# Two-layer graph network, one core: the opening's convolution by three half-rate products, weight sums on VectorE, new opening order

## The reference

```python
h = relu(layernorm(x))
c = bn1(conv1d(h^T, conv1_w)); c = relu(c)             # kernel size 1
c = bn2(conv1d(c, conv2_w, pad 8))                     # kernel size 17 along the nodes
x_conv = relu(c + h^T)^T
s = h @ w_se^T + b_se                                  # 3 coordinates a node
A = exp(-squared distances of s within a graph) * adj
x_nmp = A @ relu(h @ w_msg^T + b_msg)
x = x + GRU cell(input [x_conv, x_nmp], state h)       # w_ih, w_hh, gates r, z, n
x = x + adj @ (relu(layernorm(x)) @ L1_weight) + L1_bias
```

## Time and profile before

| | us |
|---|---|
| three runs: median (lowest, highest) | 351.57 (350.06, 353.5) |
| the profiled execution, own time | 351.87 |
| its span | 350.1 |
| busy: PE / DVE / ACT / POOL | 333.0 / 264.1 / 220.9 / 151.7 |

### The profile page before, as it was taken

One profiled execution on the slowest core, in us unless ns is written; L12 is line 12 of the kernel. 1 busy time (PEld: TensorE's weight loads), 2 busy tenths in 40 slices (PEclk: granted clock), 3 DMA queues, 4 the chain that ended last, 5 costly groups with the idle time before them and its releaser, 6 DMA issues.

```text
span 350.1 us, 6296 instructions
## 1 busy us (share of the span) xinstructions
PE 333.0 (95%) x2196; PEld 299.2 (85%) x2196; DVE 264.1 (75%) x733; ACT 220.9 (63%) x431; POOL 151.7 (43%) x130
## 2 busy tenths in 40 slices
PE   7699979999999999999999999999999999999954
PEld 5489868799989998899988998889889998999854
DVE  5597985898688977898679968899577868744672
ACT  2958635876776785677676686587667736352342
POOL 7052470025932297026912495218900593181041
PEclk9999989999999999999999999999999999999988
DMA  6900200001310031001300121002100010000001
GB/s 224 339 3 0 81 11 0 2 1 39 112 33 1 6 116 62 0 2 61 99 24 0 33 92 60 0 2 77 46 0 2 11 51 0 3 30 32 1 1 60
DMA packets 7951, 15.02 MB, mean 43 GB/s; under 512 B 1008, under 2 KB 1648, under 8 KB 7792
## 3 DMA queue, kind: packets, MB, share of 16 engines
q1 hardware_dynamic: 7776, 14.62, 12.2%
q10 hardware_dynamic: 144, 0.01, 0.0%
HBM read 10.43 MB, written 4.19 MB: 42 GB/s over the span
## 4 chain that ended last, share of the span: by engine, by line
issue 40%; POOL 27%; PE 16%; DVE 9%; ACT 6%; DMA 1%; POOLq 0%; ACTq 0%; DVEq 0%
POOL x_ring L1309 4%; POOL base L1321 3%; POOL ac L926 3%; POOL px L930 2%; POOL px L920 2%; POOL px L923 2%; POOL rs L1262 2%; POOL base L1324 2%; POOL rs L1267 2%; POOL base L1315 2%; DVE st L943 1%; DMA x_ring<-x_in 1%; PE pZ L469 1%; PE pQ L329 1%; PE pNR L305 1%
## 5 line engine op out<-in xcount | busy, mean ns | idle before, releaser
L1267 POOL TENSOR_TENSOR rs<-ve,neg_half 128x4 f32<-128x4 f32 x16 | 16.6, 1034 | 100.2 <-DVE ve L1072 100.2
L1262 POOL TENSOR_TENSOR rs<-ve,neg_half 128x8 f32<-128x8 f32 (+1 forms) x9 | 15.5, 1721 | 74.5 <-DVE ve L950 74.5
L303 PE MATMUL pP<-cx_hi,conv_hi 128*128 128x256 f32 x154 | 45.0, 292 | 0.0
L305 PE MATMUL pP<-cx_hi,conv_lo 128*128 128x256 f32 x154 | 43.4, 282 | 0.0
L304 PE MATMUL pP<-cx_lo,conv_hi 128*128 128x256 f32 x154 | 43.3, 281 | 0.0
L303 PE MATMUL pQ<-cx_hi,conv_hi 128*128 128x256 f32 x126 | 37.2, 295 | 0.0
L305 PE MATMUL pQ<-cx_hi,conv_lo 128*128 128x256 f32 x126 | 35.4, 281 | 0.0
L304 PE MATMUL pQ<-cx_lo,conv_hi 128*128 128x256 f32 x126 | 35.4, 281 | 0.0
L720 ACT ACTIVATE work<-work,nb,rs 128x128 f32<-128x128 f32 x60 | 24.8, 483 | 16.1 <-DVE nb L1076 16.1
L303 PEld LDWEIGHTS pP<-cx_hi,conv_hi 128*128 128x128 f32 x154 | 29.1, 189 | 0.3
L304 PEld LDWEIGHTS pP<-cx_lo,conv_hi 128*128 128x128 f32 x154 | 29.1, 189 | 0.3
(11 more groups left out here) (270 smaller groups left out, 1076.0 us busy)
## 6 DMA issues: line engine op xcount, KB each, us to landing
x_ring<-x_in SPq DMA_DIRECT2D x16, 256.0 KB, 2.9
adj_ring<-adj_in SPq DMA_DIRECT2D x16, 256.0 KB, 3.1
out<-x_ring SPq DMA_DIRECT2D x15, 256.0 KB, 2.0
work<-conv_in SPq DMA_DIRECT2D x1, 1088.0 KB, 7.6
x_ring<-gate_in SPq DMA_DIRECT2D x1, 576.0 KB, 7.7
out<-x_ring SPq DMA_DIRECT2D x2, 128.0 KB, 1.7
early<-early_in SPq DMA_DIRECT2D x1, 129.5 KB, 3.2
late<-late_in SPq DMA_DIRECT2D x1, 128.0 KB, 7.9
```

The source lines that it names most:

```text
L303: pe.matmul(acc, w_hi, m_hi, start=start, stop=False)
L305: return pe.matmul(acc, w_lo, m_hi, start=False, stop=stop)
L1262: pool.tensor_tensor(rs1[:, lane], ve1[:, lane], neg_half[:, lane], ALU.pow).then_inc(rs1_set, 1)
L1267: pool.tensor_tensor(rs2[g % 2][:], ve2[g % 2][:], neg_half[:, 0:GG], ALU.pow).then_inc(rs2_set, 1)
```

## The change

**Convolution of groups 0 and 1.** `direct` goes. Three products at half rate take its place, each of eight taps: `even_tap` (even weights on even minus odd phases, into `pQ`), `sum_tap` (sums of even and odd weights on the odd phases, into `pP`), `odd_tap` (odd weights on the next even minus the odd phases, into `pP` again, once `with_sum` has taken the second product's result out of `pP` into `base[0]` and `base[1]`), and tap 16 once for each bank. The differences are made on DVE (`less_odd`, `next_less_odd`), the four pairs of phases split by `split_hi_first(k)` and `split_lo_first(k)`.

**Weights.** `sum_phases` leaves POOL; `sum_odd` (`M21`, 1024 columns) and `sum_halves` (`M12` 1024, `M22` 512) are on DVE. Weights are split in seven parts, not six, in the same total. `W_SUMS` says which sums a part waits for.

**Order.** `opening()` of PE, ACT and DVE is written anew: the fronts of groups 2 and 3 move ahead of much of the convolution; the third product comes last. POOL's `scale1([2, 3])` no longer waits for `cxlo_set` 2, and the sums are gone from between it and `pre`. `split_hi(1, k)` stands in another place and order, `FIRST_ORDER`, and waits for the product that read the place before (`FIRST_FILLS`).

```diff
-        W_PARTS = (taps(8, A0), taps(8, A2), taps(1, T16), taps(4, M22), taps(8, M12), taps(8, M21))
-        W_SUMS = (0, 0, 0, 2, 2, 3)
+        W_PARTS = (taps(4, A0), taps(4, A2), taps(1, T16), taps(8, M21), None, taps(4, M22), taps(8, M12))
+        W_SUMS = (0, 0, 0, 1, 0, 3, 2)
...
-        FIRST_ORDER = (0, 3, 4, 1, 2)
+        FIRST_ORDER = (0, 3, 1, 4, 2)
+        FIRST_FILLS = (None, 3, 4, 0, 4)
...
+            def half_rate(bank, part, w, j, start=False, stop=False):
                 w_hi, w_lo = conv_hi[:, w * D:(w + 1) * D], conv_lo[:, w * D:(w + 1) * D]
+                x = FIRST_AT[part]
+                if j % 2 == 0:
+                    parts = [(bank[:], slice(x, x + 2), j // 2)]
+                else:
+                    parts = [(bank[:, 0:CG * QN], slice(x + 1, x + 2), j // 2),
+                             (bank[:, CG * QN:], slice(x, x + 1), j // 2 + 1)]
...
+            def even_tap(j):
+                return half_rate(pQ, 0, (A0, A2)[j % 2] + j // 2, j, start=j == 0)
+
+            def sum_tap(j):
+                return half_rate(pP, 1, (M21, M23)[j % 2] + j // 2, j, start=j == 0, stop=j == 6)
+
+            def odd_tap(j):
+                return half_rate(pP, 3, (A1, A3)[j % 2] + j // 2, j, start=j == 0)
```

More of the change, by code:

```diff
@@ L494, in opening @@
                 pe.wait_ge(w_split, 1)
-                pe.wait_ge(cxlo_set, 2)
[L496 to L502, removed]
+                pe.wait_ge(cxlo_set, 1)
+                even_tap(0)
+                even_tap(2)
+                even_tap(4)
+                even_tap(6)
+                messages(1)
+                pe.wait_ge(w_split, 2)
@@ L518, in opening @@
+                half_rate(pQ, 2, T16, 8, stop=True).then_inc(f_done[3], 1)
                 conv1(3)
                 neighbour_sums(1)
-                direct(14)
                 messages(3)
                 rows_turn(2)
-                direct(3)
+                pe.wait_ge(w_split, 5)
+                pe.wait_ge(cxlo_set, 4)
+                pe.wait_ge(t0_set, 2)
+                odd_tap(0)
+                odd_tap(2)
+                rows_turn(3)
+                odd_tap(4)
                 distances(2)
-                direct(7)
@@ L526, in opening @@
-                rows_turn(3)
-                direct(11)
+                odd_tap(6)
                 distances(3)
+                odd_tap(1)
+                odd_tap(3)
                 neighbour_sums(2)
[L530 to L536, removed]
+                odd_tap(5)
@@ L537, in opening @@
+                odd_tap(7)
+                half_rate(pP, 1, T16, 8, stop=True).then_inc(f_done[4], 1)
                 gates_h(0)
@@ L838, in opening @@
                 conv_round(0, 0)
+                round_w(5)
+                round_w(6)
+                sums_hi(3)
+                conv_round(0, 1)
                 hidden_gate(0)
-                conv_round(0, 1)
                 first(4)
-                sums_hi(3)
                 reset_gate(0)
@@ L1138, in opening @@
                 normalise1([2, 3])
+                sum_odd()
+                coordinates(1)
+                split_lo_first(1)
+                shift1([2, 3])
                 split_w(2)
+                split_w(3)
                 pair_rows(0)
-                coordinates(1)
-                shift1([2, 3])
                 pair_rows(1)
+                hidden_lo(2)
                 right_rows(0)
-                hidden_lo(2)
+                next_less_odd()
                 right_rows(1)
+                split_lo_first(2)
@@ L1147, in opening @@
                 masked(0)
-                split_w(3)
+                hidden_lo(3)
+                masked(1)
                 coordinates(2)
                 split_w(4)
-                hidden_lo(3)
-                masked(1)
+                split_lo_first(3)
+                sums_lo(0)
                 pair_rows(2)
-                sums_lo(0)
+                with_sum(0)
+                with_sum(1)
+                coordinates(3)
+                pair_rows(3)
+                sums_lo(1)
                 dve.wait_ge(gate_rounded, 1)
@@ L1170, in opening @@
-                conv_lo_out(0, 0)
-                conv_out(0, 1)
+                right_rows(2)
+                right_rows(3)
+                masked(2)
+                conv_out(0, 0)
+                split_lo(1, 0)
+                masked(3)
+                normalise1([4, 5])
+                sums_lo(2)
+                conv_lo_out(0, 0)
+                sum_halves()
+                sums_lo(3)
+                conv_out(0, 1)
+                shift1([4, 5])
+                conv_lo_out(0, 1)
```

208 lines of the change are left out of this document (109 added, 99 removed).

## The result

The changed kernel takes 353.38 us (median of 20 runs, 352.36 to 354.12), the kernel before 351.59 (20 runs, 349.8 to 354.19): ratio 1.0037, 95% interval 1.0019 to 1.0055. It is 1.3 us slower, beyond the measurement's uncertainty; the forecast was 1.2 us faster, 350.4. The measured time lies inside the stated range and beside rival (b), 353.1.

A forecast was written before the change was run, and what follows sets the result against it. TensorE bounds the loop; in the opening VectorE is nearly as tight, so the walk of queues decides. The lead at `o_turn(0)`, 0.3 us or 1.25 with middle interference, gave 351.87 - 1.2 = 350.7, 350.4 against the median; range 346.5 to 353.6.

The forecast's parts named there:

- rival (b): Opening, ahead of `gates_c(0)`: new waits drop TensorE's clock, costing 1.8 us; slower, 353.1 us; chance 0.22.
- Bound and start: TensorE's loop from 70 us stays unchanged; the opening's first convolution product starts at 16.2 instead of 17.26, 1.1 us earlier.
- the walk: Opening's instructions followed in each engine's new order; it, not the product count, decides; error 1 to 2 us.
- the products' 5.6: Convolution of the opening: 26 bank-taps instead of 34, so TensorE loses 5.6 us of work.
- the sum's second half: Opening up to the loop: lead of 4.75 us at `gates_h(0)` shrinks to 0.3 at `o_turn(0)`, 1.25 with middle interference.
- The interference term: GpSimd's differences falling on VectorE's `pair_rows(3)` and `gate_lo`: between 0 and 1.9 us, taken as 0.95.
- the Trainium skill's rule: VectorE instructions with two SBUF inputs and GpSimd instructions reading SBUF exclude each other whole: full 1.9 us, time 351.3.
- The low clock: TensorE at 1.2 GHz after waiting: 1.6 us in the kernel before; 1.8 us on `gates_c(0)` if it falls there.
- Its own sign: What would show the low-clock rival: a granted clock under 0.9 in the slice at 55 to 63 us.
- (a): TensorE stays the bound: the 4.75 us lead at `gates_h(0)` reaches the loop, 346.8 us; chance 0.33 with partial forms.
- (c): Opening: only the earlier start counts, products' saving wholly idle; no change, 351.5; lower half of the forecast's 0.45.

The follow-up runs named there:

- e7: Changed kernel with GpSimd's five differences for the next step held until `pair_rows(3)` and `gate_lo` are done: 352.24 us, ratio 0.9999.
- e5: Changed kernel with unused matmuls filling TensorE's waits before `rows_turn(3)`, `distances(2)`, `gates_c(0)` and `o_turn(0)`: 352.90 us, ratio 1.0026.
- e1: Changed kernel with 13 unused matmuls filling TensorE's waits before `rows_turn(3)` and `distances(2)`: 353.71 us, ratio 1.0059.
- e10: Changed kernel with `right_rows(2)` directly behind `with_sum(1)`, `M12` and `M22` summed on GpSimd, two phase splits early: 348.85 us, ratio 0.9914.
- e11: e10 with 18 unused matmuls filling five of TensorE's waits, from `rows_turn(2)` to `o_turn(0)`: 349.01 us, ratio 0.9911.
- e6: Kernel before the change, with 8 unused matmuls filling TensorE's 1.99 us wait before `distances(3)`: 350.67 us, ratio 0.9958.
- e3: Changed kernel with `sum_halves` before `right_rows(3)` on VectorE and both weight rounds behind `decay(3)` on ScalarE: 356.15 us, ratio 1.0121.
- e12: e10 with `gate_lo` behind `right_rows(3)` on VectorE instead of before it: 349.74 us, ratio 0.9931.

## Why the prediction was wrong

**Bound and start: right.** The loop did not change, and the first product came at 15.91 (forecast 16.2). The waits of the walk stood where it put them, with the releasers it named: `right_rows(2)` behind `gate_lo`, ScalarE's wait at the 512-element weight round, the four splits ahead of `o_turn(0)`. Their sizes were off: ScalarE waited 2.72 us there, not some 4, TensorE 1.52 before `gates_c(0)`, not 2.9, and `gates_h(0)` came 1.4 us earlier, not 4 to 6. TensorE's busy time in the span fell by 4.5 us, not by the products' 5.6: the low clock lasts longer than in the kernel before, which accounts for about the other 1.1.

**The step that failed is the sum's second half**, three terms against a forecast first product of 69.81 - 1.25 = 68.56 and 71.76 measured. (1) *The interference term.* I took 0.95 us, the middle of 0 and 1.9; it was 1.05 for `sq` and 0.86 for `gate_lo`, 1.9 together. This is the end that the Trainium skill's rule gave (SBUF — State Buffer, "Who interferes with whom"), and the two rows agree. e7 takes it away and gains 1.3 us. +0.95. (2) *The low clock.* I left it out of the sum and put it into rival (b), behind `gates_n(0)`. It fell earlier, behind the 2.50 us wait before `distances(2)`, and cost `gates_h(0)` 2.2 us and the first product 1.1 (e5). In 1.52 us of waiting before `gates_c(0)` it did not fall again. +1.1. (3) *The walk itself* was 1.1 us short, worked out as the rest of 3.2. 0.9 of it is there at `distances(2)` (45.03 in e1, with a full clock, against 44.1), and it stays 1.0 at `gates_c(0)` (59.01 in e5, against 58.0). 0.6 of this is there from `distances(0)` on, which starts at 28.53, not 27.95. A likely source is GpSimd's `rs`, 2.57 us instead of 1.67, overlapping VectorE's `sum_odd` (19.04 to 20.26): VectorE then idles 0.81 us for it ahead of the weight split that TensorE waits for. I had moved a VectorE instruction with two SBUF inputs beside a GpSimd instruction and priced it at its own duration. No run moves `sum_odd` away, so this part is read from the trace and not shown, and the other 0.5 of the 1.1 stays open.

**Rivals.** (b) gave the time, 353.1, but in part by luck: its low clock came at another place and cost 1.1 us, not 1.8, and the walk was 1.1 us late for other reasons. Its own sign, a clock under 0.9 at 55 to 63 us, did not appear (1.00 there). (a) needs VectorE and ScalarE to keep up; they did not. (c) said no change; e5, without the low clock, is 0.9 us slower. The chances leaned the wrong way: 1.2 us of forecast gain rested on a mean over an uncertain collision, when the full price and one low clock behind the wait before `distances(2)` were the likelier reading.

**Where the products' 5.6 us went.** TensorE's waits took them: 6.0 us idle against 2.6 in the opening window, 3.5 against 0.4 in the 15 us after it. With the halves' sums off VectorE, `right_rows(2)` early and two splits early (e10), 3.0 us of them reach the time. Half of this is the low clock that costs nothing in e10 and 1.5 us in the kernel before: with the waits filled in both, e11 is 1.7 us faster than e6.

## What to carry to other kernels

When work is taken from the busiest engine, write down for each other engine what stands ahead of the instruction that the busy one will wait for; here three placements (`gate_lo` before `right_rows(2)`, a weight sum before `sums_hi(3)`, splits before `blend_end(0)`) held back 4.3 us of a saving of 5.6 (e10 against the changed kernel). Judge a repair in the trace at the place where it should act, and try repairs together before dropping them: alone they took 0.25% and 0.13% off the time, together 0.99%, while `gates_c(0)` moved by 2.35, 1.16 and 3.92 us. Price an instruction with two SBUF operands on VectorE that would start under one of GpSimd's differences or sums at the rest of that one, not at half of it (`sq`, `gate_lo`, and the two sums of e3).

## What the runs showed of the hardware

A low clock of TensorE moves, and the length of one wait does not tell where it falls. In e1 it did not fall behind 2.62 us and fell behind 1.94 (granted clock 0.57 from 68 to 72 us); behind the wait before the first convolution product it fell in e6's execution (2.11 us, the wait as in the kernel before) and not in that of the kernel before (2.13). In e5 and e11, with the waits filled, and in e12, with none filled and none from 36 us on over 1.34 us, it did not fall between 36 and 72 us. Its price depends on cover: 1.5 us in the kernel before (e6), nothing in e10 (e11).

GpSimd's `rs` instruction of 8 elements seems to have been held itself: 2.57 us beside `sum_odd`, 1.67 in the kernel before, where VectorE's small instructions beside it kept their 0.16 to 0.25 us.
